# A mixture-of-experts stage whose scattering DMA adds weighted rows into X in DRAM

## The reference

```
x = x + attention(...)                      # layer 0; layer 1: x = x + gnn(...)
h = norm(x)                                 # layer 0: RMS, layer 1: layer norm
p = softmax(h @ router)                     # 8 values a node
w, e = top_k(p, 2);  w = w / w.sum(-1)
x = x + sum_k w[k] * expert[e[k]](h)        # layer 1's experts add a bias of their own, b2
```

## Time and profile before

| | |
|---|---|
| median of 3 runs | 972.86 us (970.52 to 976.18) |
| profiled execution | 975.67 us, its span 973.5 us |
| mean granted TensorE clock | 0.949 of full speed |
| TensorE busy | 892.7 us, 92% of the span |
| DVE, ACT, GpSimd busy | 447.8, 281.1, 182.1 us |
| layer 0's blocks | about 180 to 317 us, a scatter every 7.70 us |
| layer 1's blocks | about 414 to 484 us, a scatter every 3.73 us where nothing disturbs |
| reads of DRAM, writes | 106.11 MB, 13.36 MB |

### The profile page before, as it was taken

The page is one execution under the profiler, slowest core; times in us unless marked ns, Lnnn a source line. Parts: engine busy times, 40 slices in busy tenths (PEclk is TensorE's granted clock), DMA queues, the critical chain, the costliest instruction groups (busy, mean ns, idle before and its releaser), DMA issues.

```text
span 973.5 us, 15475 instructions
## 1 busy us (share of the span) xinstructions
PE 892.7 (92%) x5638; PEld 710.7 (73%) x5638; DVE 447.8 (46%) x1433; ACT 281.1 (29%) x625; POOL 182.1 (19%) x177
## 2 busy tenths in 40 slices
PE   6999998999999999999996778999999999899897
PEld 4776656889999877889875667777887554665665
DVE  7988555522222421632278976423434142340623
ACT  5111263122222114233347853332111111114210
POOL 2201000122221200045427751000101100000231
PEclk9999899999999999899988979999998899799899
DMA  8303001288885603159241000353100000320696
GB/s 296 142 2 92 1 1 38 96 303 315 320 325 192 235 1 130 54 187 322 98 164 68 1 1 1 130 192 120 45 1 14 19 1 1 130 96 35 206 344 230
DMA packets 28007, 120.42 MB, mean 124 GB/s; under 512 B 5401, under 2 KB 10032, under 8 KB 20132
## 3 DMA queue, kind: packets, MB, share of 16 engines
q1 hardware_dynamic: 22362, 104.39, 30.1%
q0 software_dynamic: 5280, 14.95, 4.6%
q10 hardware_dynamic: 295, 0.14, 0.1%
HBM read 106.11 MB, written 13.36 MB: 123 GB/s over the span
## 4 chain that ended last, share of the span: by engine, by line
PE 71%; DVE 15%; DMA 5%; issue 5%; ACT 2%; DVEq 1%; POOL 1%; SPq 0%; POOLq 0%; ACTq 0%
PE PS L817 8%; PE PS L473 6%; PE PS L441 5%; PE PS L832 5%; PE PS L884 4%; PE PS L868 4%; PE PS L485 4%; PE PS L552 4%; PE PS L627 2%; PE PS L908 2%; PE PS L959 2%; PE PS L948 2%; PE PS L1268 2%; DMA HT<-flat_rows,route 2%; DVE ring L1991 2%
## 5 line engine op out<-in xcount | busy, mean ns | idle before, releaser
L441 PE MATMUL PS<-const 128*128 128x128 f32 x674 | 92.8, 299 | 5.8 <-DVE X L1358 2.1
L441 PEld LDWEIGHTS PS<-const 128*128 128x128 f32 x674 | 88.2, 212 | 10.2 <-DVE X L1358 2.9
L817 PE MATMUL PS<-HT,ring 128*128 128x128 f32 x680 | 79.1, 275 | 3.3 <-DVE HT L1512 1.7
L817 PEld LDWEIGHTS PS<-HT,ring 128*128 128x128 f32 x680 | 78.4, 192 | 4.6 <-issue 3.9
L2655 POOL TENSOR_TENSOR col<-col,power 125x4 f32<-125x4 f32 (+2 forms) x13 | 11.9, 917 | 315.4 <-DVE col L1351 226.5
L2715 POOL DMA_INDIRECT slot_rows<-ST,route x41 | 41.4, 1010 | 151.1 <-ACT ST L2429 96.0
L2753 POOL TENSOR_TENSOR arena<-arena,ring 125x625 f32<-125x625 f32 x40 | 55.7, 1416 | 34.3 <-ACT arena L2517 30.1
L1911 DVE TENSOR_TENSOR HT<-HT,PS 128x256 f32<-128x256 f32 (+1 forms) x51 | 19.1, 376 | 89.8 <-ACT HT L2418 71.6
L627 PE MATMUL PS<-HT 125*128 125x126 bf16 x530 | 41.7, 230 | 6.8 <-DVE HT L1722 6.7
L1049 PE MATMUL PS<-w,HT 125*64 125x125 f32 x400 | 30.3, 305 | 18.0 <-DVE w L2010 18.0
L832 PE MATMUL PS<-ring,HT 128*128 128x256 f32 x204 | 46.8, 380 | 0.0
(11 more groups left out here) (472 smaller groups left out, 1712.3 us busy)
## 6 DMA issues: line engine op xcount, KB each, us to landing
ring<-in_experts SPq DMA_DIRECT2D x17, 1386.0 KB
ring<-in_experts SPq DMA_DIRECT2D x17, 768.0 KB, 6.0
ring<-in_experts SPq DMA_DIRECT2D x11, 1026.0 KB
arena<-in_experts SPq DMA_DIRECT2D x10, 1024.0 KB
ring<-in_experts SPq DMA_DIRECT2D x7, 1024.0 KB, 7.6
arena<-in_experts SPq DMA_DIRECT2D x6, 1026.0 KB
arena<-in_gnn SPq DMA_DIRECT2D x5, 1024.0 KB, 5.9
ring<-in_experts SPq DMA_DIRECT2D x8, 513.0 KB, 3.7
```

The costliest lines, as they stand in the source:

```text
L441: pe.matmul(PS[:, bank, 0:128], ident, ident, start=True, stop=True)
L817: mm = pe.matmul(PS[:, bank, at:at + SLOTS], both[:, j, k, m * 128:(m + 1) * 128], xs[0][i % 2][:, k, :], start=(k == 0), stop=(k == KD - 1))
```

## The change

In layers 0 and 1 the normed rows go to DRAM once, and X itself is written to the first 625 rows of `slot_rows`. A pair's weight is looked up by slot: DVE splits each float32 weight into three bf16 parts, spreads them over the blocks, TensorE's `weight_table` sums them into a table of slots by blocks, and DVE's `take_weights` adds the three parts. The copy of an expert's result from PSUM multiplies each row by its slot's weight. The scatter then adds its rows to the rows of X in DRAM. Since both pairs of a node go to one row, each scatter waits until the one before has landed, and the first until X has been written. The read-back goes straight into X, one row per node, and `mix_rows` only takes statistics; in layer 1 it adds the bias from PSUM to each tile after it has landed. In layer 0, X + XN is computed behind the transposes. The numbers of useless matmuls change from 62 to 44 and from 27 to 14. The semaphore `router_in` is gone, its load counts into `small_in`; `x_biased` is now `x_added`. Layer 3 keeps its way.

```diff
@@ TensorE
+            def weight_table(L):
+                pairs = PICKS[L] * NT
+                pe.wait_ge(weights_made, 3 * NTH[L] + 1)
+                for a in range(pairs):
+                    mm = pe.matmul(PS[:, 4, 0:3 * BLOCKS[L]], in_slot(L)[:, a, :],
+                                   third_values(L)[:, a].rearrange("p j n -> p (j n)"), start=(a == 0), stop=(a == pairs - 1))
+                mm.then_inc(weights_made, 1)
@@ layer0_moe, and in layer1_moe before its down(0)
                 emptied()
                 stay_busy(7, 6)
+                weight_table(0)
                 down(0)
@@ layer1_gnn, layer2_gnn
-                transposes(XN, busy=62)
+                transposes(XN, busy=44)
-                transposes(XN, busy=27)
+                transposes(XN, busy=14)
@@ DVE, mix_rows
                     dve.wait_ge(mixed_in[t], 32 * (NTH[L] + 1))
-                    for k in range(PICKS[L]):
-                        ins = dve.scalar_tensor_tensor(X[:, t, :], mixed[L][:, t, k, :], mixes(L)[:, t, k:k + 1],
-                                                       X[:, t, :], ALU.mult, ALU.add)
...
+                    if L == 1:
+                        b, at = (bank(), 0) if t < NT - 1 else (b, D)
...
+                        taken(dve.tensor_tensor(X[:, t, :], X[:, t, :], PS[0:TP, b, at:at + D], ALU.add))
+                        own_banks()
+                    ins = dve.bn_stats(stats[:, t, :], X[:, t, :])
@@ DVE, new
+            def take_weights(L):
+                dve.wait_ge(weights_made, 3 * NTH[L] + 2)
+                dve.tensor_reduce(slot_weight[:, 0:BLOCKS[L]], PS[:, 4, 0:3 * BLOCKS[L]].rearrange("p (j n) -> p n j", j=3),
+                                  AX.X, ALU.add).then_inc(weights_made, 1)
@@ DVE, routing, after mix
+                    whole = mix[:, 0:pairs]
+                    for j in range(3):
+                        link(dve.tensor_copy(thirds[:, :, j], whole))
+                        if j < 2:
+                            link(dve.tensor_tensor(left_over[j], whole, thirds[:, :, j], ALU.subtract))
+                            whole = left_over[j]
+                    dve.tensor_tensor(third_values(L), in_block_.unsqueeze(2).broadcast_to([TP, pairs, 3, blocks]),
+                                      thirds.unsqueeze(3).broadcast_to([TP, pairs, 3, blocks]),
+                                      ALU.mult).then_inc(weights_made, 1)
@@ DVE, layer0_moe
                 rms_norm()
-                dve.tensor_tensor(X[:, :, :], X[:, :, :], XN[:, :, :], ALU.add).then_inc(chain, 1)
-                n["chain"] += 1
                 take_transposes(XT, scale=COLS(cols, "ln2_w"))
+                dve.tensor_tensor(X[:, :, :], X[:, :, :], XN[:, :, :], ALU.add).then_inc(x_added, 1)
...
+                    if i == 0:
+                        take_weights(0)
@@ DVE, layer1_moe
                 routing(1)
+                take_weights(1)
...
-                        dve.tensor_copy(ys[1][:, b, :], PS[:, 5 + (i - 1) % 2, 0:D]).then_inc(ys_taken, 1)
-                for t in range(NT):
-                    b = bank()
-                    taken(dve.tensor_tensor(X[:, t, :], X[:, t, :], PS[0:TP, b, 0:D], ALU.add))
-                own_banks()
+                        if i == 1:
+                            dve.wait_ge(weights_made, 6)
+                        dve.tensor_scalar(ys[1][:, b, :], PS[:, 5 + (i - 1) % 2, 0:D], slot_weight[:, i - 1:i], None,
+                                          ALU.mult).then_inc(ys_taken, 1)
@@ ScalarE, layer0_moe
-                        act.activation(ys[0][:, b, :], PS[:, 5 + (i - 1) % 2, 0:D],
-                                       ACT.Copy).then_inc(ys_taken, 1)
+                        if i == 1:
+                            act.wait_ge(weights_made, 3)
+                        act.activation(ys[0][:, b, :], PS[:, 5 + (i - 1) % 2, 0:D], ACT.Identity,
+                                       scale=slot_weight[:, i - 1:i]).then_inc(ys_taken, 1)
@@ GpSimd, scatter, for layers 0 and 1
                 pool.wait_ge(ys_taken, BASE[L] + i + 1)
...
+                if i:
+                    pool.wait_ge(ys_out[(i - 1) % AHEAD[L]], rounds(L, i - 1))
+                else:
+                    pool.wait_ge(copy_out, 64 + 32 * (NTH[L] + 1))
                 pool.indirect_dma_start(slot_rows[L], bass.IndirectOffsetOnAxis(to_row[:, i:i + 1], 0),
-                                        ys[L][:, b, :], None, bounds_check=2 * N + BLOCKS[L] * SLOTS - 1,
-                                        oob_is_err=False).then_inc(ys_out[b], 16)
+                                        ys[L][:, b, :], None, bounds_check=N + BLOCKS[L] * SLOTS - 1,
+                                        compute_op=ALU.add).then_inc(ys_out[b], 16)
@@ SyncE, rows_out and rows_back
-                for k in range(2):
-                    for p0, p1 in ((0, 120), (120, TP)):
-                        sp.dma_start(copies[p0:p1, :, k, :], ROOT[p0:p1, :, :]).then_inc(flat_out, 16)
+                for p0, p1 in ((0, 120), (120, TP)):
+                    sp.dma_start(normed[p0:p1], ROOT[p0:p1]).then_inc(flat_out, 16)
+                sp.wait_ge(x_added, 1)
+                for p0, p1 in ((0, 120), (120, TP)):
+                    sp.dma_start(start[p0:p1], X[p0:p1]).then_inc(copy_out, 16)
...
-                    sp.dma_start(mixed[L][0:120, t], back[0:120, t]).then_inc(mixed_in[t], 16)
+                    sp.dma_start(read_back[L][0:120, t], back[0:120, t]).then_inc(mixed_in[t], 16)
```

More of the change, by code:

```diff
@@ L182, in build @@
         out_done = sem("out_done")
+        weights_made = sem("weights_made")
         act_full, act_free = sem("act_full"), sem("act_free")
@@ L348, in build @@
         share = view(MB, 1824, TP, NT)
+        left_over = [view(MB, 1840 + 2 * NT * j, TP, 2 * NT) for j in range(2)]
+        thirds = view(MB, 1880, TP, 3 * NT).bitcast(BF16).rearrange("p (a j) -> p a j", j=3)
+        third_rows = view(MB, 1920, TP, 3 * NT * MOST).bitcast(BF16)
         spare = arena[:, 2 * NT * N:]
-        mixed = {L: spare[0:TP, 0:2 * NT * D].rearrange("p (t k d) -> p t k d", t=NT, k=2) for L in (0, 1)}
-        mixed[3] = ROOT[:, :, :].unsqueeze(2)
+        read_back = {0: X, 1: X, 3: ROOT}
         xs_rows = {0: view(spare, 2 * NT * D, 128, 4, D), 1: view(spare, 2 * NT * D, 128, 4, D),
@@ L369, in build @@
         swish = view(HT, 2 * M0 * 128, 128, M0, SLOTS)
-        flat_rows = {L: nc.dram_tensor(f"flat_rows{L}", [PICKS[L] * N, HID3 if L == 3 else D], F32).ap() for L in AHEAD}
-        slot_rows = {L: nc.dram_tensor(f"slot_rows{L}", [2 * N + BLOCKS[L] * SLOTS, D], F32).ap() for L in AHEAD}
+        flat_rows = {L: nc.dram_tensor(f"flat_rows{L}", [N, HID3 if L == 3 else D], F32).ap() for L in AHEAD}
+        slot_rows = {L: nc.dram_tensor(f"slot_rows{L}", [N + BLOCKS[L] * SLOTS, D], F32).ap() for L in AHEAD}
         limits = N // PER[3]
@@ L539, in bias2 @@
                 for t in range(NT):
-                    bank = dve_bank()
+                    at = 0
+                    if which == 1 and t == NT - 1:
+                        n["v"] += 1
+                        at = D
+                    else:
+                        bank = dve_bank()
                     if t in (0, 4):
                         pe.wait_ge(act_free, n["a"] - (t == 0))
-                    pe.matmul(PS[0:TP, bank, 0:D], combT[:, t * TP:(t + 1) * TP], b2s[:, (which - 1) * D:which * D],
+                    pe.matmul(PS[0:TP, bank, at:at + D], combT[:, t * TP:(t + 1) * TP], b2s[:, (which - 1) * D:which * D],
                               start=True, stop=True).then_inc(dve_full, 1)
@@ L2854, in rows_out @@
             def rows_out(L):
-                copies = flat_rows[L].rearrange("(p t k) d -> p t k d", t=NT, k=2)
-                for k in range(2):
-                    for p0, p1 in ((0, 120), (120, TP)):
-                        sp.dma_start(copies[p0:p1, :, k, :], ROOT[p0:p1, :, :]).then_inc(flat_out, 16)
+                normed, start = (v[0:N, :].rearrange("(p t) d -> p t d", t=NT) for v in (flat_rows[L], slot_rows[L]))
+                for p0, p1 in ((0, 120), (120, TP)):
[3 more added lines that the diff above has]
+                    sp.dma_start(start[p0:p1], X[p0:p1]).then_inc(copy_out, 16)
             def rows_back(L):
```

74 lines of the change are left out of this document (42 added, 32 removed).

## The result

The kernel after the change takes 1000.16 us (median; 997.69 to 1003.55), the kernel before, run beside it, 971.69 us. The ratio is 1.0296, with a 95% interval from 1.0262 to 1.033: 3% slower. The prediction was 973.6 us, with a range up to 983.

The account below looks back on a forecast made before the run. TensorE, busy for 92% of the span, was taken to bound the kernel outside the stages' ends. Terms -0.9 + 1.1 + 1.75 - 4.3 - 2.9 + 0.65 + 5.3 = +0.7 us on the median 972.86 gave 973.6, range 967 to 983.

Parts of the forecast that it names:

- X + XN moved: Layer 0's start: the router's matmuls start earlier, the add being hidden under them; -0.9 us.
- The weights in three parts: Before down(0): DVE's extra small operations and larger product delay it; +1.1 us in layer 0, +1.75 in layer 1.
- Read-back: Stage ends: fewer bytes read and less DVE mixing in layer 0, shorter filler in layer 1; -4.3 and -2.9 us.
- The filler of 44: Useless matmuls at layer 0's end: finish at 326.6, no later than the first transpose could start; no cost.
- Layer 0's chain: Scatters in layer 0: no wait in the middle; the last waits 0.4 us and lands 0.25 later; +0.65 us.
- Layer 1's chain: Scatters in layer 1: loaded adding landings of 4.25 us set the pace for ten gaps; +5.3 us with the end.
- the chain binds hard: Slower rival, layer 1: loaded landings of 5 us, +12.9 with the end, total +8.3, 981.2 us; chance 0.25.
- one window: Layer 1, 435.5 to 437.5 us: 96 packets moved, so a loaded plain scatter lands 3.8 to 4.8 us after its start.
- the bound of 5 us for the landing: Adding scatter's upper bound: a read and a write one after the other, about 5 us; 3.0 was taken.

Follow-up runs that it names:

- e7: Changed kernel, layer 1's odd blocks added into a second tensor of rows, each scatter waiting for the last but one: 979.05 us, ratio 1.0114.
- e1: Kernel before, with each plain scatter of layers 0 and 1 waiting until the one before has landed: 981.7 us, ratio 1.0136.
- e4: Changed kernel without layer 1's ten late loads of experts' weights, adding and waiting kept, another output: 981.8 us, ratio 1.0111.
- e8: Kernel before with each gather of layers 0 and 1 issued one scatter earlier: 968.38 us, ratio 0.9994.
- e10: Kernel before with chained plain scatters (as e1), without layer 1's ten late weight loads, another output: 970.55 us, ratio 0.9993.
- e2: Kernel before with scatters that add to separate, pre-filled rows and don't wait for each other, another output: 975.64 us, ratio 1.0052.
- e3: Changed kernel with scatters overwriting instead of adding, waits kept, so the output isn't the sum: 979.88 us, ratio 1.009.
- e6: Changed kernel with every gather of layers 0 and 1 issued a block earlier: 1002.14 us, ratio 1.0336.

## Why the prediction was wrong

**X + XN moved: right.** Predicted -0.9, measured -0.87: the logits start 2.69 us after the normed rows, where it was 3.56.

**The weights in three parts: right in layer 1** (+1.75 predicted, +1.59 measured; the product took 0.69 us where I took 0.7). In layer 0 the stretch up to the last eviction has +0.2 in the prediction and -0.10 in the traces.

**Read-back: right in kind.** Layer 0 gave 5.1 us where I had 4.3, layer 1 gave 3.27 where I had 2.9. The filler of 44 ended at 323.5, 2.97 us before layer 1's transposes started. I had its end by the rate of before, but the scatter ahead of it was late, which I had costed at 0.65 us. So its early end did cost something: after these 2.97 idle us the ten transposes ran at a granted clock of 0.50 (326.4 to 329.0 us) and took 2.35 us, where they had taken 1.79.

**Layer 0's chain: wrong in size.** +0.65 predicted; the last scatter starts 2.26 us later behind its eviction and lands 1.11 us later: +3.4. The last two scatters stand 4.76 us apart. I had put the landing at 3.0 and nothing for the hand-over. That landings don't set the pace in its middle came true in the sum: 121.76 us against 119.62 from the first scatter to the last, and the difference is the last gap's (4.76 for 2.59). But it was near. I had a landing at 6.3 us at most; adding ones took 5.7 to 7.9 there, and with the hand-over that passes the 7.71 us of a block. Gaps of 8.3 to 8.5 us that end on a landing alternate with gaps of 6.9 to 7.1 that make up for them, and in e7's trace they weren't made up for.

**Layer 1's chain: the step that failed.** The prediction has it as "I take 4.25 for the adding one, loaded. Ten gaps of 4.25 put scatter 10 at 467.8", a term of +5.3 with the end. It measured +30.85 +1.10 = +32.0. The mechanism was the right one: GpSimd waits on `slot_rows`, and the gathers come late behind it. But a gap is the landing and the hand-over, and I took it for the landing alone. The first ten gaps took 62.24 us, 24.2 more than before (I had +3.5): 6.22 us each, of which 5.37 are landing, for my 4.25, and 0.86 the hand-over, for my nothing. The last six took 27.71 us, 6.7 more than before (I had +1.3, for the last one only). Three sizes were wrong:

1. *An adding scatter.* I took 3.0 unloaded, "near the plain one". It is 3.54 to 3.86. Its issue is 0.57 us longer (1.58 against 1.01), and the rest comes behind the issue.
2. *The hand-over.* I reckoned the pace as the landing. But from a landing to the start of the next scatter there are another 0.82 to 0.86 us, so the unloaded pace is 3.25 us for plain scatters (e1, where the landing is 2.4) and 4.45 for adding ones (508.41 to 512.86, landing 3.63). This alone is above the 3.73 of a block. The rival "the chain binds hard" decided "from about 4.7" by my count, and the pace of e4, with no loads at all, is 4.7.
3. *The load.* I set the loaded landing 1.25 us above the unloaded one, from one window in which the packets of a scatter and of a gather moved, and argued that a slower pace thins the loads. The landings under load ran from 3.8 to 8.84 us. My window was read rightly, but it held one scatter at the edge of the loads: that of 432.65 landed after 4.27 us in the trace of before. For the seven behind it (436.38 to 459.49) the last updates that this trace holds come 5.8 to 7.5 us after the start; some of its records are missing, so they can only have landed later. e8's trace, with the scatters of the kernel before and the gathers a block earlier, has them all. Its DMA view of 434 to 459 us gives the issues (count, median us to landing):

```profile
slot_rows<-ST,route POOLq DMA_INDIRECT x7, 7.0
```

So plain scatters that nobody waits for take 7.0 us under load. That a chained pace thins the load is right in direction (5.37 in the mean of the first ten after, adding and all), but it starts from 7.0 and not from 4.3.

So 16 x (4.7 - 3.73) = 15.5 us are the unloaded chain (e4 against e10: 16.1), and 15.0 are the loads. The range of 983 ended at a landing of 5.2 us for ten gaps. The mean gap was 89.95 / 16 = 5.6 us, for all sixteen. The rival "binds hard" (981.2 us, 0.25) went the right way with a term of 12.9 for the 32.0. I had put the gaps after scatter 10 at nothing because the weights are loaded by then; but they too are longer than a block, once the unloaded pace is.

**What would have shown it.** The trace of before had the hand-over. TensorE and GpSimd both waited for layer 0's last eviction; TensorE's filler started at 316.56, GpSimd's scatter at 317.28. That is 0.72 us in which GpSimd had nothing left to wait for, hidden in the row's "1.61 idle before". The landings under load were there too, as far as its records go, in the blocks from 436 us on. The adding issue and landing no row of before showed; but the bound of 5 us for the landing was in the text, and with it and 0.72 for the hand-over the gaps would have come to 16 x (5.72 - 3.73) = 32 us. That it meets the 30.85 so well is partly luck: the landings were 4.75 us in the mean, but from 3.5 to 8.84. The text had that landing and let it go into ten gaps without the hand-over.

**The landing by a formula.** The Trainium skill's "DMA: Bandwidth & Descriptors" (Anatomy of one DMA) gives 2.3 us for such a scatter by its fit: near the plain landings of 2.44 and 2.75, and 1.2 us and more under the adding ones. The Trainium skill's "Collectives: The Full Stack" (the bandwidth ceiling) says of the adding step of a collective that it is slower for its second source. The trace agrees in direction: the unloaded landing is 1.1 us later, of which 0.57 is the issue, and the queue shows three times the packets.

## What to carry to other kernels

Before independent transfers are made into a chain, work out the chain's pace as start to landing plus the hand-over from landing to next start, and set it against the time of a block: above it, every block pays the difference; a little under it, a burst of loads in the same stretch takes it over. Take the landing from several transfers in the middle of the load and not from one at its edge. Saved work at a stage's end is paid once; a wait inside a loop of blocks is paid at every one, so multiply first. Two targets in turn, with the wait on the last but one, bring back most of it.

## What the runs showed of the hardware

- An indirect scatter of 128 rows of 1 KB that adds keeps GpSimd 1.58 us at its issue, a plain one 1.01, with or without a chain (e1, e2).
- It leaves 144 packets on GpSimd's queue where a plain one leaves 48. For the last but one scatter of the kernel after, with nothing else moving, the DMA view of 508.4 to 512.8 us (share of the 16 engines in 40 slices; packets, MB, share of the queue; issues) reads:

```profile
DMA  0000000000000000000996996999600000000000
...
q0 software_dynamic: 144, 0.13, 25.7%
...
slot_rows<-ST,route POOLq DMA_INDIRECT x1, 3.6
```

Its packets move in ten of the 40 slices, about 1.1 us from 510.5 on; 2.1 us of the 3.6 pass before the first of them.
- Under load, the same view of 451.3 to 461.0 us shows what the scatter that took 8.84 us shared the engines with:

```profile
q1 hardware_dynamic: 370, 2.77, 76.8%
q0 software_dynamic: 211, 0.29, 17.1%
```

The packets of the weights are 7.5 KB in the mean (2.77 MB by 370), and GpSimd's are small. The Trainium skill's "DMA: Bandwidth & Descriptors" (Queues, rings and completion order) says that each engine goes round its queues packet by packet. By this, three times the packets meet three times the large ones. The runs bear this out only in part. Chained, adding landings stretch further under load (to 8.84 us) than plain ones (6.7 in e1). Not chained, they hardly differ: the same view of e2, whose scatters add, has for 434 to 459 us

```profile
slot_rows<-ST,route POOLq DMA_INDIRECT x7, 7.2
```

against the 7.0 of e8's plain ones. That the loads stretch a landing is shown (e4, e10); by what means wasn't tried. Smaller loads would be a test.
- From a landing that GpSimd waits for to the start of its next scatter there are 0.82 to 0.86 us in layer 1 after and in e1, e3, e4 and e6, plain or adding, loaded or not (once in each 1.15 to 1.17).
- TensorE's granted clock, 1.00 through these blocks before, fell to 0.58 in the 5 us after an idle stretch of 5 us, and stayed at 1.00 in e4, where TensorE was idle for 1.4 of 10 us in short pieces.
